# A graph network on one core: a relational layer's tail done in two parts, its fills moved, and a packing step moved behind the first layer

## The chip, the cores and the metric

The kernel runs on one core of a Trainium2 chip. The metric is the device time of one execution, in microseconds (us).

## What is computed

Four message-passing layers over 100,000 nodes of 32 features and 25,000 edges that come sorted by destination. Each layer normalizes, applies relu, aggregates over edges and adds to x:

```
h = relu(layernorm(x)); x = x + L0(h)   # norm * (segment_sum((norm*h)[src]) + norm*h)
h = relu(layernorm(x)); x = x + L1(h)   # four Chebyshev steps: feat += segment_sum(w * feat[dst])
h = relu(layernorm(x)); x = x + L2(h)   # relational attention, 86 edge types:
    msg = sum_b w_comp[etype, b] * (h[src] @ weight[b])
    a   = tanh(relu(sum((h[src]@A1 + b1) * (h[dst]@A2 + b2 + rel[etype])) / sqrt(32)))
    L2  = relu(segment_sum(a * msg, dst) + h[src of the node's last edge] @ self_loop)   # 0 without edges
h = relu(layernorm(x)); x = x + L3(h)   # ten steps: h = 0.9 * norm * segment_sum((norm*h)[src], dst) + 0.1 * h0
```

A node without edges gets only the parts of its own row, and in the last layer 0.1 * h0 goes into the output.

## The kernel before

**Columns.** The edges lie in 196 columns (`EC`) of 128 edges, one edge to a partition, so a table of all edges' rows is 128 x 6272 numbers (196 x 32). A segment sum is 32 running sums over the columns of a partition (`tensor_tensor_scan`, one for each feature) and one carry from partition to partition by TensorE.

**Rows in and out.** POOL fetches rows (`gather`, L1783) and writes rows (`scatter`, L1789) by indirect DMAs, one column of 128 rows each; an index beyond the bound drops its row. Nodes without edges ("dense" rows) pass through DVE and ScalarE in halves, and are written by plain DMAs of ScalarE's queue.

**The linked nodes.** After the segment sums, few rows matter to the later steps of layers 1 and 3: rows of nodes with edges whose source also has edges. Their lists are ranked, packed by matmuls against one-hot tiles (`spread`, L1118; `gathered_up`, L1148; `keyed`, L1028; `ranked`, L1049) and padded to 46, 12 and 4 columns. In the last layer the remaining steps work on one 128 x 128 matrix of links: a round of matmuls (L2271), two small DVE instructions, and again ("the rounds").

**Order of the work around the change.** Every engine runs its own program, in the written order, and waits on semaphores.

- DVE, layer 0: the lists of edges are made; the lists of nodes with several edges and of the edges that follow are packed (L1284 to L1295); then come dense halves, the norm of the sources (`source_norm`, L1349), `first_layer` (L1382) in three parts of the columns, and layer 1.
- Layer 2 is a loop of 49 turns of four columns (`l2_turns`, L1624). PE, ScalarE and DVE hand tiles to each other in it; DVE multiplies 128 x 512 products (L589) and reduces them over the 16 bases (L1602, `add_bases`), which raises the semaphore `l2_done` once a column. Behind the loop stands a tail over all 196 columns: the gate, the running sums (`segment_sums`, L982), the carry, relu and residual in pieces of 40 columns (`with_fed`, L633), then the copy of the rows into the table `own` (`OWNT`, L1646), which SP stores; zeros into `kept` (L1650, raises `l3_zero`); the layernorm; the table `first`, which SP also stores; and the rows `OUT` that are to be filled in.
- POOL during layer 2: 196 scatters of the source nodes' rows ("sends", L1901 to L1904), 12 of them free, the others one for each column done (`SENDS_AHEAD`). Behind the tail: 46 gathers from `own`, 46 from `first`, 38 fills, 12 + 12 gathers of the second list, 18 fills, 4 gathers of link rows; then the rounds with six fills in each of seven (`FILLS_TURN`, L1931); 4 scatters; 98 more fills; 46 + 12 last scatters. A "fill" (`fills`, L1912) writes a column of 0.1 * h0 plus residual for destination nodes that no later step touches; there are 196.

```
for k in range(L3_STEPS - 2):
    pool.wait_ge(s["link_turn_in"], k + 1)
    if k < L3_STEPS - 3:
        fills(early + FILLS_TURN * k, FILLS_TURN)
```

Of the kernel before, what the change touches and what calls it, by code (L numbers as in the profile page):

```python
# [8 lines left out]
D = 32  # L9
# [44 lines left out]
SENDS_AHEAD = 12  # L54
FILLS_LISTING, FILLS_PLACING, FILLS_TURN = 38, 18, 6
# [3 lines left out]
FEEDS = tuple((k, min(k + FEED, EC)) for k in range(0, EC, FEED))  # L59
UNROLL = 4  # L60
# [4 lines left out]
def build(nc, x, src, dst, etype, theta, w_basis, w_comp, w_self, a1t, a1b, a2t, a2b, rel, out):  # L65
# [33 lines left out]
    with ctx:  # L99
# [33 lines left out]
        def col(n):  # L133
            return c[n][:, 0:EC]
# [152 lines left out]
        v_at += W3 * ROWW  # L287
        V3, V3T = (rows(z_t[:, v_at + k * W3 * D:v_at + (k + 1) * W3 * D]) for k in range(2))
# [30 lines left out]
        def edge_layout(tile, at, nv, xw, wo):  # L319
# [92 lines left out]
            outd_scattered""".split()  # L412
# [31 lines left out]
        def _(sp):  # L444
# [116 lines left out]
            listed_tables("l3", OWNT, ((0, EC),))  # L561
# [22 lines left out]
        def _(dve):  # L584
# [697 lines left out]
            lead0, given0 = c["sq_out"][:, 100:100 + W0], c["sq_out"][:, 150:150 + W0]  # L1282
            link.many([ts(lead0, lead_p, -1.0, None, ALU.add), ts(given0, edge_p, -1.0, None, ALU.add)])
            spread(place0, receives, (ptr0, lead0, given0), W0, WM, MULTI)  # L1284
            ids = c["sq_out"][:, 0:3 * WM].rearrange("p (q v) -> p q v", v=3)
            gathered_up(ids, WM, 3, c["tmp"])
            many = slice(WS, W1)
            keyed(ids, WM, (pf0[:, many], owni[:, many], dst_slot[:, many]), contc[:, many], headc[:, many], wc[:], nohome[:, many])
            link(ts(valid1[:, many], ids[:, :, 1], 0.5, None, ALU.is_gt))

            place0 = ranked(follows, W0, WF)
            spread(place0, follows, (lead0, given0), W0, WF, FOLLOWING)
            ids = c["sq_out"][:, 0:2 * WF].rearrange("p (q v) -> p q v", v=2)
            gathered_up(ids, WF, 2, c["tmp"])
            pointers(ids, c["st2"][:, 0:2 * WF].rearrange("p (q v) -> p q v", v=2), ((0, leadF), (1, edgeF)))  # L1295
# [61 lines left out]
            dve.wait_ge(s["sums_scattered"], 16 * W0)  # L1357
            link(V.memset(kept[:, 0:kept_w], 0.0))
            V.memset(kept_keys, FAR).then_inc(s["l1_zero"], 1)
# [32 lines left out]
            for part in range(1, len(XS_PARTS)):  # L1392
                source_norm(part)
                first_layer(*XS_PARTS[part])
            dve.wait_ge(s["l1_own_ready"], len(XS_PARTS))
# [161 lines left out]
            link(V.tensor_copy(col("dst_out"), icols["outD"][:]))  # L1557

# [75 lines left out]
            ts(col("score"), col("score"), float(D) ** -0.5, 0.0, ALU.mult, ALU.max).then_inc(s["tail_ready"], 1)  # L1634
            dve.wait_ge(s["gate_made"], 1)
            link(tt(M, Z, bc(MEAN), ALU.mult))
            segment_sums(link, M, s["carry_in"], s["carry_out"], 1, None)
            V.memset(small[:, 2:3], 0.0).then_inc(s["tail_ready"], 1)

            def add_self(lo, hi, h):  # L1640
# [15 lines left out]
            link(tt(icols["outF"][:], col("dst_out"), col("tmp"), ALU.add))
            dve.wait_ge(s["outs_scattered"], 16 * EC)
            with_fed(lambda lo, hi, h: V.scalar_tensor_tensor(out=OUT[:, lo:hi, :], in0=h, scalar=ALPHA, in1=XD[:, lo:hi, :],
                                                              op0=ALU.mult, op1=ALU.add))
# [3 lines left out]
            dve.wait_ge(s["l3_first_ready"], 1)  # L1663
            dve.wait_ge(s["l3_first_stored"], 16)
            dve.wait_ge(s["l3_own_stored"], 16)
# [84 lines left out]
            with dve.Else():  # L1750
                ch = Chain(dve, s["dve"], before_end)
                dve.wait_ge(s["l3_listed_in"], 16 * w2)
                dve.wait_ge(s["l3_listed_stored"], 16)
                dve.wait_ge(s["l3_second_in"], 16 * w2)
                dve.wait_ge(s["l3_back_clear"], 16)
                layernorm_of(XD, F, Z, ch, roots("root_in", "root_out", root_count[0]))
# [20 lines left out]
        def _(pool):  # L1777
# [128 lines left out]
            pool.wait_ge(s["l3_own_stored"], 16)  # L1906
            gather(lambda k: OWN1[:, k, :], tables["l3", "own"], own3l, last[P * EC], s["l3_own_in"], W)
            pool.wait_ge(s["l3_first_stored"], 16)
# [6 lines left out]
            pool.wait_ge(s["d_rows_ready"], 1)  # L1915
            fills(0, FILLS_LISTING)
# [4 lines left out]
            early = FILLS_LISTING + FILLS_PLACING  # L1921
            fills(FILLS_LISTING, FILLS_PLACING)
            pool.wait_ge(s["fits_set"], 1)
            longest = pool.value_load(fits[0:1, 1:2], min_val=0, max_val=EC)
            with pool.If(longest <= XW):
                pool.wait_ge(s["l3_third_stored"], 16)
                gather(lambda q: GOT[:, q, :], links_dram, from3, last[P * w2], s["l3_third_in"], W3)
# [11 lines left out]
                pool.wait_ge(s["dfull_out"], 16 * EC)  # L1939
                pool.wait_ge(s["dc_out"], 16 * (W + w2))  # L1940
            with pool.Else():
# [7 lines left out]
                pool.wait_ge(s["dfull_out"], 16 * (FILLS_LISTING + FILLS_PLACING))  # L1949
# [6 lines left out]
        def _(act):  # L1956
# [21 lines left out]
            def feed(source):  # L1978

                act.wait_ge(s["normed"], norms[0])  # L1980
                for k, (lo, hi) in enumerate(FEEDS):
# [122 lines left out]
            l2_turns(0, EC // 4)  # L2104
            act.wait_ge(s["tail_ready"], 1)
            S.activation(MEAN, col("score"), ACT.Tanh).then_inc(s["gate_made"], 1)
            act.wait_ge(s["l2_cs"], EC)
            act.wait_ge(s["tail_ready"], 2)
            feed(XS)
            norm(XS, Z)  # L2110
            feed(Z)
# [191 lines left out]
```

## Time and profile before

| | |
|---|---|
| median of 3 runs | 2469.23 us (2468.75 to 2469.87) |
| profiled execution: its own time | 2470.35 us |
| its span in the profile | 2468.6 us |
| busy: DVE, POOL, ACT, PE, of the span | 1818.3 (74%), 1419.5 (58%), 388.7 (16%), 327.9 (13%) us |
| granted TensorE clock, mean over the span | 0.847 |

The span runs from the first to the last instruction that the profiler saw; the own time of that execution is 1.75 us longer. An engine's busy time says little by itself here: DVE and POOL are the bound in turn, each in stages of its own, so the profile has to be read by stage.

### The profile page before, as it was taken

The numbers are of one execution on the slowest core, as the hardware profiler recorded it, in microseconds if no ns is written. First come the engines' busy times: TensorE is split into PE (matmuls) and PEld (weight loads), VectorE is DVE, ScalarE is ACT, GpSimd is POOL, SyncE is SP. The second block draws the span as 40 slices with busy tenths as digits, with TensorE's granted clock in tenths as the row PEclk, the third lists the DMA queues.
The fourth block names the chain that finished last, engine by engine and source line by source line (L and its number), as shares of the span: only waits on it lengthen the run. The fifth ranks groups of instructions, "written<-read, shape, count | busy, mean of one in ns | idle before, by whom it ended". The sixth has DMA issues, their size and how long they took to land.

```text
span 2468.6 us, 12924 instructions
## 1 busy us (share of the span) xinstructions
PE 327.9 (13%) x2316; PEld 243.5 (10%) x2316; DVE 1818.3 (74%) x3200; ACT 388.7 (16%) x1275; POOL 1419.5 (58%) x1426
## 2 busy tenths in 40 slices
PE   0000000201100000010000001066764000034000
PEld 0000000101000000000000001044442000034000
DVE  8998989988699995971889989999999952321000
ACT  0000001010022121200112200177774210000000
POOL 6666776371776047306777720366662177777776
PEclk9999999999999999999999999976666555555555
DMA  1001003000221125100122220000000120100000
GB/s 21 17 9 29 12 16 119 6 12 2 96 66 32 51 67 178 42 34 10 63 71 62 84 77 0 3 8 8 8 8 4 59 69 10 35 12 11 8 8 8
DMA packets 57643, 88.37 MB, mean 36 GB/s; under 512 B 26387, under 2 KB 49864, under 8 KB 56184
## 3 DMA queue, kind: packets, MB, share of 16 engines
q0 software_dynamic: 44864, 19.00, 5.1%
q1 hardware_dynamic: 6872, 43.31, 4.5%
q10 hardware_dynamic: 5856, 25.60, 2.7%
q14 instruction: 46, 0.38, 0.1%
q8 instruction: 5, 0.08, 0.0%
HBM read 37.41 MB, written 54.76 MB: 37 GB/s over the span
## 4 chain that ended last, share of the span: by engine, by line
DVE 59%; POOL 15%; issue 12%; PE 6%; DMA 3%; ACT 2%; DVEq 0%; ACTq 0%; SPq 0%; POOLq 0%
POOL out L1789 9%; DVE mf L589 9%; POOL mf L1783 6%; DVE pay L589 4%; DVE psum L1321 4%; DVE pay L1307 4%; DVE psum L1306 3%; DVE outs L589 3%; DVE z L589 2%; PE psum L2271 2%; DVE z L1602 2%; DVE psum L618 2%; PE psum L2234 1%; DVE mf L1311 1%; DVE xs L1311 1%
## 5 line engine op out<-in xcount | busy, mean ns | idle before, releaser
L1789 POOL DMA_INDIRECT out<-outs,i_src x196 | 200.3, 1022 | 236.9 <-DVE outs L1578 109.2
L1783 POOL DMA_INDIRECT xd<-in_x,i_dst x196 | 205.2, 1047 | 109.7 <-DVE mf L589 55.5
L1783 POOL DMA_INDIRECT xs<-in_x,i_outS x196 | 195.9, 999 | 68.9 <-issue 56.4
L1789 POOL DMA_INDIRECT out<-outs,i_srcX x196 | 199.3, 1017 | 62.3 <-issue 57.6
L589 DVE TENSOR_TENSOR mf<-mf 128x128 f32<-128x128 f32 (+6 forms) x582 | 181.0, 348 | 10.5
L2005 ACT ACTIVATE pay<-pay 128x1248 f32<-128x1248 f32 (+1 forms) x63 | 75.6, 1199 | 647.4 <-DVE pay L1307 627.2
L589 DVE TENSOR_TENSOR pay<-psum,pay 128x512 f32<-128x512 f32 x196 | 130.4, 684 | 16.8 <-ACT pay L2095 14.7
L1602 DVE TENSOR_REDUCE z<-pay 128x512 f32 (+1 forms) x196 | 132.3, 675 | 0.0
L2234 PE MATMUL psum<-pay 128*128 128x512 f16 x196 | 102.7, 524 | 89.3 <-ACT pay L2080 55.6
L1783 POOL DMA_INDIRECT mf<-l_own_rows,lists x50 | 49.8, 996 | 111.9 <-DMA l_own_rows<-xs 97.0
L1783 POOL DMA_INDIRECT mf<-l_own_rows,ptr x46 | 45.9, 998 | 99.1 <-DMA l_own_rows<-pay 85.4
L1321 DVE SCALAR_TENSOR_TENSOR psum<-pay,psum 128x1248 f32<-128x1248 f32 (+1 forms) x63 | 88.7, 1407 | 2.2
L1789 POOL DMA_INDIRECT sums_by_edge<-mf,edge x46 | 45.3, 985 | 66.0 <-DVE mf L589 52.3
L1783 POOL DMA_INDIRECT mf<-l_second_rows,nsrc x26 | 26.0, 998 | 98.0 <-DMA l_second_rows<-mf 90.4
L2178 PE MATMUL psum<-lists,lower 128*128 128x32 f32 x4 | 1.3, 412 | 587.1 <-DVE lists L1189 587.1
L1306 DVE TENSOR_REDUCE psum<-outs 128x39 f32<-128x1248 f32 (+1 forms) x45 | 62.0, 1378 | 22.3 <-DMA outs<-in_x 21.8
L1783 POOL DMA_INDIRECT mf<-payload_by_dst,edge x46 | 45.8, 996 | 48.0 <-DVE mf L1225 34.3
L589 DVE TENSOR_TENSOR outs<-outs,psum 128x1248 f32<-128x1248 f32 (+2 forms) x55 | 68.5, 1258 | 1.6
L2224 PE MATMUL psum<-ident,pay 128*128 128x128 f16 x197 | 54.9, 279 | 92.0 <-ACT pay L2072 92.0
L1307 DVE SCALAR_TENSOR_TENSOR pay<-psum,outs 128x1248 f32<-128x1248 f32 (+1 forms) x45 | 62.1, 1381 | 1.6
L2148 PE MATMUL psum<-small,upper 128*128 128x1 f32 x18 | 5.3, 363 | 405.9 <-DVE small L1002 405.9
L2178 PEld LDWEIGHTS psum<-lists,lower 128*128 128x128 f32 x4 | 1.0, 312 | 587.4 <-DVE lists L1189 587.4
(521 smaller groups left out, 2726.2 us busy)
## 6 DMA issues: line engine op xcount, KB each, us to landing
outs<-in_x ACTq DMA_DIRECT2D x14, 624.0 KB, 5.4
out<-outs ACTq DMA_DIRECT2D x14, 624.0 KB, 3.0
l_first_rows<-mf SPq DMA_DIRECT2D x2, 3234.0 KB, 9.8
z<-in_x ACTq DMA_DIRECT2D x6, 624.0 KB, 6.0
out<-z ACTq DMA_DIRECT2D x6, 624.0 KB, 2.9
l_own_rows<-pay SPq DMA_DIRECT2D x1, 3430.0 KB, 9.5
payload_by_dst<-z SPq DMA_DIRECT2D x1, 3234.0 KB, 9.5
sums_by_edge<-z SPq DMA_DIRECT2D x1, 3234.0 KB, 17.3
```

The costliest lines, as they stand in the source:

```text
L589: return V.tensor_tensor(o, a, b, op)
L618: link(V.tensor_reduce(total, xin, AX.X, ALU.add))
L1306: chain(V.tensor_reduce(dense_m[b][0:pn, 0:cn], X3, AX.X, ALU.add))
L1307: V.scalar_tensor_tensor(out=rows(dxc[b][0:pn, 0:w]), in0=bc(dense_m[b][0:pn, 0:cn]), scalar=-1.0 / D, in1=X3, op0=ALU.mult, op1=ALU.add). ...
L1311: V.tensor_reduce(dst2[b][0:pn, 0:cn], rows(dsq[b][0:pn, 0:w]), AX.X, ALU.add).then_inc(s["dense_var"], 1)
L1321: chain(V.scalar_tensor_tensor(out=rows(h), in0=rows(dxc[b][0:pn, 0:w]), scalar=0.0, in1=bc(scale), op0=ALU.max, op1=ALU.mult))
L1602: V.tensor_reduce(Z[:, bass.ds(t, 1), :], prod[slot].rearrange("p (o b) -> p o b", b=NBAS).unsqueeze(1), AX.X, ALU.add).then_inc(s["l2_don ...
L1783: G.indirect_dma_start(out=dest(k), out_offset=None, in_=table, in_offset=bass.IndirectOffsetOnAxis(ap=idx[:, k:k + 1], axis=0), bounds_ch ...
L1789: G.indirect_dma_start(out=table, out_offset=bass.IndirectOffsetOnAxis(ap=idx[:, k:k + 1], axis=0), in_=source(k), in_offset=None, bounds_ ...
L2005: S.activation(dsq[b][0:pn, 0:w], dxc[b][0:pn, 0:w], ACT.Square).then_inc(s["dense_sq"], 1)
L2224: T.transpose(XXTp[b % 2], xxc[b], ident16[:])
L2234: T.matmul(PWm[b % 2], xxt[b], w_both, start=True, stop=True)
```

## The change

1. **Packing.** The packing of the two lists, and the zeros into layer 1's `kept`, move from ahead of the dense halves to behind the three `first_layer` parts. A copy of one small column (`place_m`) keeps what the packing reads.
2. **Two parts.** The loop of layer 2 is split after 24 turns (`CUT_TURN`), that is, after 96 columns (`CUT`). Between the two loops DVE does the tail for those 96 columns (slice `A`): the gate, running sums, relu and residual, the rows of `own` (in the tile `XSW`), the layernorm, the rows to be filled in (in `Z`) and the rows of `first`. Behind the second loop it does the other 100 columns (slice `B`), with column 95 (`HEADC`) again in the slice `BH`. The first segment of a partition, whose sum lacks the carry from the partition before, may end in the first part; its one row goes out by three extra scatters of one column each (into `own`, into `first`, and as a fill). Their indices, and those of the fills, are made by 19 short instructions ahead of layer 2.
3. **POOL's order.** Of the 196 sends 38 are free instead of 12, 40 are spread over DVE's work between the loops, and the others follow the columns done. Then 96 fills are issued, paced by the columns done, before the gathers from `own` start.
4. **No fills between the rounds.** `FILLS_TURN` is 0: of the 100 fills that are left, 38 and 18 stand where they stood, and 44 behind the rounds.

```diff
-SENDS_AHEAD = 12
-FILLS_LISTING, FILLS_PLACING, FILLS_TURN = 38, 18, 6
+SENDS_AHEAD = 38
+FILLS_LISTING, FILLS_PLACING, FILLS_TURN = 38, 18, 0
+CUT_TURN = 24
+CUT = 4 * CUT_TURN
+HEADC = CUT - 1
+SENDS_BETWEEN = 40
+OWN_BEFORE_HEAD = 36
...
-            spread(place0, receives, (ptr0, lead0, given0), W0, WM, MULTI)
...
-            pointers(ids, c["st2"][:, 0:2 * WF].rearrange("p (q v) -> p q v", v=2), ((0, leadF), (1, edgeF)))
+            place_m = end0
+            link(V.tensor_copy(place_m, place0))
...
                 source_norm(part)
                 first_layer(*XS_PARTS[part])
...
+            spread(place_m, receives, (ptr0, lead0, given0), W0, WM, MULTI)
...
+            V.memset(kept_keys, FAR).then_inc(s["l1_zero"], 1)
...
-            l2_turns(0, EC // 4)
+            l2_turns(0, CUT_TURN)
+            dve.wait_ge(s["l2_done"], CUT + 2)
...
+            gated(MA, A, 1)
+            running_sums(MA, A)
...
+            link(tt(Z[:, A, :], Z[:, A, :], CUR[:, A, :], ALU.add))
...
+            for given, out_row in ((Z, head_sum), (XD, head_own[:, 0:D])):
+                link(tt(MA, given[:, A, :], bc(ends), ALU.mult))
+                link(V.tensor_reduce(out_row, MA.rearrange("p c f -> p f c"), AX.X, ALU.add))
+            link(V.scalar_tensor_tensor(out=XD[:, A, :], in0=Z[:, A, :], scalar=0.0, in1=XD[:, A, :], op0=ALU.max, op1=ALU.add))
...
+            layernorm(XD[:, A, :], HA, MA, w=WA)
...
+            l2_turns(CUT_TURN, EC // 4)
...
+            gated(MB, B, 2)
...
+            running_sums(MB, B)
...
             for k in range(EC):
-                if k >= SENDS_AHEAD:
+                if k >= CUT + SENDS_AHEAD + SENDS_BETWEEN:
+                    pool.wait_ge(s["l2_done"], 3 + k - SENDS_AHEAD - SENDS_BETWEEN)
...
+            pool.wait_ge(s["d_rows_ready"], 1)
+            for k in range(CUT):
+                behind = EC - CUT - SENDS_AHEAD - SENDS_BETWEEN + k
+                pool.wait_ge(s["l2_done"], 2 + min(CUT + behind + 1, EC))
+                scatter(out, lambda q: Z[:, q, :], icols["outF"], last[N], s["dfull_out"], 1, k)
             pool.wait_ge(s["l3_zero"], 1)
```

POOL's program before, from the sends of layer 2 to the end (`out<-outs,i_src` are the sends, `i_srcX` the fills, `l_own_rows` and `l_first_rows` the tables, `z<-l_link_rows` the link rows of the rounds):

```order
L1789 DMA out<-outs,i_src 100000x32 x196
L1783 DMA mf<-l_own_rows,ptr 128x35 x46
L1783 DMA mf<-l_first_rows,ptr 128x33 x46
L1789 DMA out<-outs,i_srcX 100000x32 x38
...
L1789 DMA out<-outs,i_srcX 100000x32 x18
...
L1783 DMA z<-l_link_rows,linksi 128x33 x4
L1789 DMA out<-outs,i_srcX 100000x32 x42
L1789 DMA l_third_rows<-z,linksi 1536x32 x4
L1789 DMA out<-outs,i_srcX 100000x32 x98
```

The same stretch of POOL's program in the changed kernel:

```order
L1902 DMA out<-outs,i_src 100000x32 x196
L1902 DMA out<-z,i_srcX 100000x32 x96
L1902 DMA l_own_rows<-pay,edge 25088x35
L1896 DMA mf<-l_own_rows,ptr 128x35 x36
L1902 DMA l_first_rows<-mf,edge 25088x33
L1896 DMA mf<-l_own_rows,ptr 128x35 x10
...
L1902 DMA out<-outs,edge 100000x32
L1902 DMA out<-outs,i_srcX 100000x32 x38
...
L1896 DMA z<-l_link_rows,linksi 128x33 x4
L1902 DMA l_third_rows<-z,linksi 1536x32 x4
L1902 DMA out<-outs,i_srcX 100000x32 x44
```

96 fills moved ahead of the gathers from `own`, the 42 between the rounds are gone from there, and 44 instead of 98 stand behind; three scatters of one column are new.

DVE's program between the two loops of the changed kernel, where the kernel before has nothing (`score` and `psum` are the gate, `xd` the residual, `xs` the copy for `own`):

```order
L618 TENSOR_SCALAR score<-score 128x96
L615 TENSOR_TENSOR mf<-z,psum 128x3072
L1684 SCALAR_TENSOR_TENSOR z<-cont,mf 128x96 x32
...
L615 TENSOR_TENSOR mf<-z,tmp 128x3072
L1705 TENSOR_REDUCE chosen<-mf 128x32
...
L1706 SCALAR_TENSOR_TENSOR xd<-z,xd 128x3072
...
L1708 COPY xs<-xd 128x96x32
...
L656 SCALAR_TENSOR_TENSOR mf<-mf,psum 128x3072
L1712 SCALAR_TENSOR_TENSOR z<-mf,xd 128x3072
```

Instructions that ran over 196 columns behind the loop now run over 96 here, and over 100 or 101 behind the second loop.

## Rows read from the trace of the kernel before

**Rows 1.** Page part 4: shares of the chain that ended last, by engine.

```profile
DVE 59%; POOL 15%; issue 12%; PE 6%; DMA 3%; ACT 2%; DVEq 0%; ACTq 0%; SPq 0%; POOLq 0%
```

**Rows 2.** Windows: us; busy us (count) of PE, PEld, DVE, ACT, POOL; PEclk; DMA.

```profile
608.20:649.60 41.40, 6.98 (x98) 6.09 (x98) 32.21 (x67) 0.00 (x0) 31.32 (x32) 1.00 0.06 12
...
1596.70:1893.40 296.70, 202.46 (x1571) 133.52 (x1571) 279.78 (x543) 210.21 (x1084) 180.55 (x184) 0.70 0.04 7
1893.40:1951.10 57.70, 0.64 (x2) 0.50 (x2) 54.61 (x56) 6.32 (x6) 0.00 (x0) 0.50 0.00 0
...
2198.20:2253.10 54.90, 49.12 (x224) 48.17 (x224) 4.49 (x21) 0.00 (x0) 41.31 (x42) 0.50 0.04 8
2258.40:2385.20 126.80, 0.64 (x2) 0.50 (x2) 6.01 (x38) 0.00 (x0) 96.85 (x98) 0.50 0.05 9
```

**Rows 3.** Timeline, own rows to first gather: start, us, instruction, idle before.

```profile
1951.14 0.33 SPq L508 DMA_DIRECT2D l_own_rows<-pay  x1
1951.94 3.69 DVE L1650 MEMSET mf<- 128x4352 f32 x1 [0.82 <-issue]
...
1961.45 1.05 POOL L1783 DMA_INDIRECT mf<-l_own_rows,ptr  x1 [85.41 <-DMA l_own_rows<-pay]
```

**Rows 4.** Waits of POOL from 1961.4 on: total us, times, longest us.

```profile
POOL out L1789 <- issue: 75.2, 247, 0.3
```

**Rows 5.** Timeline of layer 1's start: the norm, POOL's gather, its first reader.

```profile
883.50 6.70 DVE L618 TENSOR_REDUCE psum<-xs 128x196 f32<-128x6272 f32 x1
887.60 0.99 POOL L1783 DMA_INDIRECT mf<-l_own_rows,lists  x1 [96.96 <-DMA l_own_rows<-xs]
...
1047.61 0.20 DVE L1422 COPY kc<-mf 128x50 f32<-128x50 f32 x1
```

**Rows 6.** Groups by form, DVE, 1893.2 to 1951.2: busy us, mean ns, idle.

```profile
L984 DVE TENSOR_TENSOR_SCAN z<-cont,mf 128x196 f32<-128x196 f32 x32 | 14.7, 542 | 0.0
L589 DVE TENSOR_TENSOR mf<-z,psum 128x6272 f32<-128x6272 f32 x1 | 6.7, 6689 | 0.4 <-ACT psum L2106 0.4
L1642 DVE SCALAR_TENSOR_TENSOR xd<-psum,xd 128x1280 f32<-128x1280 f32 x4 | 6.0, 1491 | 0.1
...
L589 DVE TENSOR_TENSOR z<-z,psum 128x2112 f32<-128x2112 f32 x2 | 4.7, 2353 | 0.1
L1646 DVE COPY pay<-xd 128x6272 f32<-128x6272 f32 x1 | 3.4, 3428 | 0.0
...
L592 DVE TENSOR_SCALAR score<-score 128x196 f32<-128x196 f32 x1 | 0.3, 262 | 0.1
```

**Rows 7.** Groups by form, DVE, 807 to 824: a layernorm over 104 columns.

```profile
L618 DVE TENSOR_REDUCE psum<-xs 128x104 f32<-128x3328 f32 x1 | 3.6, 3628 | 0.0
...
L628 DVE RECIPROCAL psum<-sq_out 128x104 f32<-128x104 f32 x1 | 0.8, 810 | 0.4 <-ACT sq_out L1975 0.4
```

**Rows 8.** Timeline: DVE's running sums over 46 columns, POOL's scatters beside them.

```profile
2083.37 4.60 DVE L1188 TENSOR_TENSOR_SCAN pay<-lists,mf 128x46 f32<-128x46 f32 x30
2084.47 4.34 POOL L1789 DMA_INDIRECT out<-outs,i_srcX  x1 [0.30 <-issue]
...
2089.12 0.98 POOL L1789 DMA_INDIRECT out<-outs,i_srcX  x1 [0.30 <-issue]
```

**Rows 9.** Timeline of DVE at the start of layer 2's loop.

```profile
1600.87 0.69 DVE L589 TENSOR_TENSOR pay<-psum,pay 128x512 f32<-128x512 f32 x1 [3.29 <-ACT pay L2095]
```

**Rows 10.** Windows of 10 us within layer 2's loop (columns as Rows 2).

```profile
1690.00:1700.00 10.00, 8.03 (x57) 5.31 (x55) 9.30 (x18) 6.66 (x38) 6.64 (x7) 0.51 0.04 8
1700.00:1710.00 10.00, 5.70 (x51) 3.76 (x50) 9.62 (x20) 7.37 (x38) 6.60 (x7) 0.83 0.04 8
```

**Rows 11.** Chain in order of time: start, us, the link rows' last transfer.

```profile
2195.28 2.35 DMA z<-l_link_rows,linksi
```

**Rows 12.** Timeline of one round of the links' matrix.

```profile
2198.06 7.04 PE L2271 MATMUL psum<-z,xs 128*128 128x32 f32 x32 [23.33 <-DVE small L1733]
...
2205.14 0.29 DVE L589 TENSOR_TENSOR z<-psum,z 128x128 f32<-128x128 f32 x1 [7.13 <-PE psum L2271]
```

More of the change, by code:

```diff
@@ L59, with feeds_of @@
 FEEDS = tuple((k, min(k + FEED, EC)) for k in range(0, EC, FEED))
+def feeds_of(first, last):
+    return tuple((k, min(k + FEED, last)) for k in range(first, last, FEED))
 UNROLL = 4
@@ L287, in build @@
         v_at += W3 * ROWW
+        head_own, head_sum = chosen[:, 0:OWNW], chosen[:, OWNW:OWNW + D]
+        cut_sum, cut_row = extra[:, 2 * W1:2 * W1 + D], extra[:, 2 * W1 + D:2 * W1 + 2 * D]
+        head_fill, head_row = edge0[:, 0:1], edge0[:, 1:2]
+        WA, WB = CUT, EC - HEADC
+        A, B, BH = slice(0, CUT), slice(CUT, EC), slice(HEADC, EC)
+        MA, HA = rows(mf[:, 0:WA * D]), rows(mf[:, WA * ROWW:WA * ROWW + WA * D])
+        HB = rows(z_t[:, CUT * D:CUT * D + WB * D])
+        assert WA * (ROWW + D) <= (CUT + 4) * 2 * D and CUT * D + WB * D <= EC * PAYLOAD
         V3, V3T = (rows(z_t[:, v_at + k * W3 * D:v_at + (k + 1) * W3 * D]) for k in range(2))
@@ L559, in _ @@
                 sp.dma_start(by_dst, xd_t[:]).then_inc(s["y_table"], 16)
-            listed_tables("l3", OWNT, ((0, EC),))
+            own_rows = tables["l3", "own"].rearrange("(p c) w -> p c w", p=P)
+            first_rows = tables["l3", "first"].rearrange("(p c) w -> p (c w)", p=P)
+            for k, (own, part) in enumerate(((XSW, A), (OWNT, B))):
+                sp.wait_ge(s["l3_own_ready"], k + 1)
+                sp.dma_start(own_rows[:, part, :], own[:, part, :]).then_inc(s["l3_own_stored"], 16)
+                sp.wait_ge(s["l3_first_ready"], k + 1)
+                span = slice(part.start * ROWW, part.stop * ROWW)
+                sp.dma_start(first_rows[:, span], first_f[:, span]).then_inc(s["l3_first_stored"], 16)
             sp.wait_ge(s["l3_cleared"], 1)
@@ L631, in layernorm, with with_fed @@
                 dve.wait_ge(s["normed"], norms[0])
-            def with_fed(step):
-                for k, (lo, hi) in enumerate(FEEDS):
+            def with_fed(step, parts=FEEDS):
+                for k, (lo, hi) in enumerate(parts):
                     dve.wait_ge(s["fed"], feeds[0] + 1)
@@ L1557, in _ @@
             link(V.tensor_copy(col("dst_out"), icols["outD"][:]))
+            ends, free = c["tmp"][:, A], c["tmp2"][:, 0:EC]
+            link(ts(free, col("kn"), FAR / 2, FAR, ALU.is_lt, ALU.mult))
+            link(tt(free, free, col("dst_out"), ALU.add))
+            link(V.tensor_copy(icols["outF"][:, B], free[:, B]))
+            link(V.scalar_tensor_tensor(out=icols["outF"][:, A], in0=c["head"][:, A], scalar=FAR, in1=free[:, A], op0=ALU.mult, op1=ALU.add))
+            link(tt(ends, c["head"][:, A], c["head"][:, 1:CUT + 1], ALU.subtract))
+            none, picked, found_at = c["st2"][:, 0:1], c["st1"][:, A], c["st2"][:, 1:2]
+            link(V.tensor_reduce(none, ends, AX.X, ALU.add))
+            link(ts(none, none, -FAR, FAR, ALU.mult, ALU.add))
+            for given, out_index in ((free[:, A], head_fill), (c["linear"][:, A], head_row)):
+                link(tt(picked, ends, given, ALU.mult))
+                link(V.tensor_reduce(found_at, picked, AX.X, ALU.add))
+                link(tt(out_index, found_at, none, ALU.add))
+            for k, name in enumerate(("dis", "kn", "dst_out")):
+                link(tt(picked, ends, c[name][:, A], ALU.mult))
+                link(V.tensor_reduce(head_own[:, D + k:D + k + 1], picked, AX.X, ALU.add))
             dve.wait_ge(s["dense_out"], 16 * (DCHUNKS + 1))
@@ L1629, in l2_turns, with gated, running_sums @@
                     l2_turn(last - 1, 0, False)
-            l2_turns(0, EC // 4)
+            def gated(out, part, number):
+                ts(c["score"][:, part], c["score"][:, part], float(D) ** -0.5, 0.0, ALU.mult, ALU.max).then_inc(s["tail_ready"], 1)
+                dve.wait_ge(s["gate_made"], number)
+                link(tt(out, Z[:, part, :], bc(MEAN[:, part]), ALU.mult))
+            def running_sums(m, part):
+                link.many([V.tensor_tensor_scan(Z[:, part, f], c["cont"][:, part], m[:, :, f], 0.0, ALU.mult, ALU.add) for f in range(D)])
@@ new lines, in own_rows @@
+            def own_rows(own, part):
+                link(V.tensor_copy(own[:, part, D], c["dis"][:, part]))
+                link(V.tensor_copy(own[:, part, D + 2], c["dst_out"][:, part]))
+                link(V.tensor_copy(own[:, part, D + 1], c["kn"][:, part]))
+            l2_turns(0, CUT_TURN)
+            dve.wait_ge(s["l2_scored"], CUT_TURN + 1)
+            dve.wait_ge(s["l2_done"], CUT + 2)
+            dve.wait_ge(s["l2_xy"], CUT_TURN + 1)
+            marks["cut"] = link.n
+            gated(MA, A, 1)
@@ new lines, in _ @@
+            link(V.scalar_tensor_tensor(out=XD[:, A, :], in0=Z[:, A, :], scalar=0.0, in1=XD[:, A, :], op0=ALU.max, op1=ALU.add))
+            link(V.tensor_copy(cut_row, XD[:, HEADC, :]))
+            link(V.tensor_copy(XSW[:, A, 0:D], XD[:, A, :]))
+            own_rows(XSW, A)
+            V.memset(small[:, 2:3], 0.0).then_inc(s["l3_own_ready"], 1)
+            layernorm(XD[:, A, :], HA, MA, w=WA)
+            V.scalar_tensor_tensor(out=Z[:, A, :], in0=HA, scalar=ALPHA, in1=XD[:, A, :],
+                                   op0=ALU.mult, op1=ALU.add).then_inc(s["d_rows_ready"], 1)
@@ L1638, in _ @@
+            dve.wait_ge(s["carry_out"], 1)
+            for lo, hi in SUM_CUT[1:]:
+                lo = max(lo, CUT)
+                added = rows(ADDED[:, 0:(hi - lo) * D])
+                link(tt(added, bf(CAR, hi - lo), bc(c["head"][:, lo:hi]), ALU.mult))
+                link(tt(Z[:, lo:hi, :], Z[:, lo:hi, :], added, ALU.add))
             V.memset(small[:, 2:3], 0.0).then_inc(s["tail_ready"], 1)
+            dve.wait_ge(s["l3_own_stored"], 16)
+            link(tt(head_sum, head_sum, CAR, ALU.add))
@@ L1640, in add_self @@
+            link(V.scalar_tensor_tensor(out=XD[:, HEADC, :], in0=head_sum, scalar=0.0, in1=head_own[:, 0:D], op0=ALU.max, op1=ALU.add))
             def add_self(lo, hi, h):
@@ L1913, in fills @@
                 scatter(out, lambda q: OUT[:, q, :], icols["outF"], last[N], s["dfull_out"], n, first)
-            pool.wait_ge(s["d_rows_ready"], 1)
-            fills(0, FILLS_LISTING)
+            pool.wait_ge(s["d_rows_ready"], 2)
+            scatter(out, lambda q: OUT[:, HEADC, :], head_fill, last[N], s["dfull_out"], 1)
+            fills(CUT, FILLS_LISTING)
             pool.wait_ge(s["l3_second_stored"], 16)
```

133 lines of the change are left out of this document (84 added, 49 removed).

## The prediction

> **What bounds the kernel now.** I read the chain that ended last first, then the windows by stage, then the groups and timelines of the stages that the change touches. The chain gives DVE 59% and POOL 15% [rows 1], and the windows show where one hands over to the other [rows 2]. Up to 1951.1 DVE sets the pace: it is busy 279.8 of 296.7 us in layer 2's loop and 54.6 of 57.7 in the tail. At 1951.1 the rows of `own` are complete and their store begins; 10.3 us later POOL's first gather starts [rows 3]. From there POOL works without a break to the end: before its scatters it only waits for issue, 0.3 us at the longest [rows 4], and the fills behind the rounds come at 126.8/98 = 1.294 us each [rows 2]. So two things count: when the first gather from `own` starts, and how many transfers POOL has to issue after it.
>
> All sums go against the profiled execution's own time, 2470.35 us (span 2468.6); the median of the runs is 2469.23, 1.12 lower, and I take that off at the end.
>
> **Packing moved: 0.2 us.** The stretch is 41.4 us with DVE busy 32.2; the rest is its waits for PE between its own steps [rows 2]. In the new place DVE does the same work with the same waits. Added is one small copy, 0.2. POOL's gather from layer 1's `own` starts 4.1 us behind the work that stands ahead of the norm, since it waits for a store [rows 5]; that store will now lie beside the packing. But the gather's first reader is DVE at 1047.6, without idle time [rows 5], so 160 us cover it; were that cover gone, its shift would count in full. The trace has no row for the swapped order, so I bound it by these 4.1 us to either side and take 0.
>
> **Indices ahead of layer 2: +5.0.** 19 short instructions at 0.262 [rows 6]; DVE is the pace there. Two of them leave a place beside POOL's gathers, where they cost nothing.
>
> **The work between the loops: +58.** Counted in DVE's program: 13 passes over 96 x 32 = 3072 numbers (gate; self row; two products and two reduces for the leading segment; relu with residual; four of the layernorm; fills; `first`). A pass costs 3.628/3328 x 3072 = 3.35 [rows 7], together 43.5. 32 running sums: 4.60/30 = 0.153 each over 46 columns [rows 8] and 14.7/32 = 0.459 over 196 [rows 6] give by a straight line 0.255 over 96, so 8.2. The copy for `own`: 3.43 x 96/196 = 1.7 [rows 6]. A reciprocal, 0.75 [rows 7], and nine small ones at 0.26: 3.1. ScalarE's tanh and root: 0.4 each [rows 6, 7]. Some 25 gaps of 0.035, as between DVE's instructions elsewhere: 0.9. Sum 58.2. Bounds: the two reduces walk with a stride that no row shows; between the 3.35 of a contiguous one and its double I take the former, +6.7 at most and nothing below. The second loop may begin with the 3.29 that DVE waited at the first start [rows 9]; here PE and ScalarE have 58 us to fill their tiles ahead, so I take 0, +3.3 at most.
>
> **The loop itself: 0.** PE now rests for 58 us in its middle. The granted clock swings within the loop anyway, 0.51 in one window of 10 us and 0.83 in the next (the levels are 1.2 and 2.4 GHz), while DVE is busy 9.30 and 9.62 [rows 10]. So a window at the slow level costs 0.32 in 10 us at most. For the 100 columns behind the cut, half of 296.7 = 151 us, that bounds the price at 0.032 x 151 = 4.8 if the clock stays low throughout. At the loop's mix it is 0, which I take, for the clock rises in this loop without help.
>
> **The tail behind the loop: 57.7 to 33.0, so -24.7.** Over 100 of 196 columns the gate takes 3.4 instead of 6.7, the running sums 8.4 instead of 14.7; relu and residual, two passes at 1491/1280 ns a number, 7.5 instead of 14.6; the carry, two passes at 2353/2112, 7.1 instead of 14.0; the copy 1.8 instead of 3.4 [rows 6]. Waits, 57.7 - 54.6 = 3.1 [rows 2], stay, and so do small ones, with the leading segment's 1.7.
>
> Together the rows of `own` are ready 0.2 + 5.0 + 58.2 - 24.7 = 38.7 later, near 1990.
>
> **From there to the first gather: 10.3 to 7.4, so -2.9.** Before, the store set it, 10.3 us, beside 4.5 us up to the end of the zeros into `kept` [rows 3]. Now the last store is half as long, some 5 by proportion; the zeros (4.6), then the leading segments' scatter until it has landed (2.35 for a column's transfer [rows 11]) and an issue gap set it. First gather: +35.8, near 1997.
>
> **POOL afterwards: -67.3.** Two more scatters of leading segments: 2 x 1.294 = +2.6. The gathers and the 38 + 18 fills stay. **In the rounds,** a round is 7.04 us of PE, seven times, and DVE waits for PE's last matmul each time, not for POOL [rows 12]; so the 42 fills that leave them save nothing there, and POOL will stand idle for most of 55 us. Behind the rounds 44 fills stand where 98 stood: 54 x 1.294 = -69.9. Put otherwise: of the 96 fills that leave POOL's last stretch, 42 had been free.
>
> Row against rule: PE is busy 49.1 of these 54.9 us at a granted 0.50 throughout, the level of 1.2 GHz, while it was granted 1.00 from 608 to 650, where it worked 7 of 41 us [rows 2]. So I leave the rounds at 7.04. The Trainium skill ("TensorE: Matmul & The Clock Gate", Part 1: The HAM clock gate) has it that the slow level is the default and sustained activity lifts it; by that the rounds would run at the fast level, which rival 1 works out. This trace does not agree.
>
> **Does the backlog fit?** The 96 fills are free only if POOL is through with them when the zeros are ready, near 1994.6. Some of DVE's passes hold POOL's transfers up: a scatter that takes 0.98 took 4.34 beside the running sums and ended with the last of them [rows 8]. Between the loops I put such passes at half of the 58 us, so 28 of the 40 sends get done there. 12 + 22 sends and 96 fills are left for the second loop and the tail, 1805 to 1994.6. In the loop a transfer is not held up: 180.55/184 = 0.98 [rows 2]. A column takes 1.51, so POOL catches the 12 up at 0.2 a column, in some 75 columns, and ends the loop, at 1956, with the 19 fills that wait for its end: 19 x 1.29 = 24.5, and 10 of holding up by the tail's sums, 1990.5. It fits by 4 us. That is the weakest step.
>
> **Sum:** +35.8 + 2.6 - 69.9 = -31.5: own time 2438.9, against the median 2437.7. **I predict 2438.** With the bounds above (-4.1 to +4.1, +6.7, +3.3, +4.8, not all at once) this case alone reaches from 2432 to 2450.
>
> **Rivals.**
>
> 1. *Rounds at the fast level.* PE's rest in mid-loop shifts the sequence of levels; at 2.4 GHz each round would lose up to 7.04/2, seven of them 24.6: 2413. For it: the clock moves both ways in the loop [rows 10]. Against: 0.50 through all rounds [rows 2]. Chance 0.05.
> 2. *A mild backlog.* If a transfer takes p in the second loop and tail, 130 of them and the 10 of holding up have 189.6 us; they fit up to p = 1.38. At p of 1.45 to 1.50 the first gather moves by 9 to 15: 2447 to 2453. For it: passes that hold POOL up [rows 8]. Against: 0.98 in the loop, 1.29 from start to start behind the rounds [rows 2]. Chance 0.11.
> 3. *The other side: a backlog that eats the gain.* The first gather stands behind all 96 fills in POOL's program, so each that is late counts in full. From p = 1.62 (130 x 1.62 + 10 is 31 over) the kernel is slower than before; at 1.75 the first gather is 48 late: 2486. It needs DVE's 128 x 512 products to hold POOL up once it is driven closer, which the loop before doesn't show. Chance 0.04.
> 4. *The fills between the rounds weren't free,* if they slowed PE or DVE there. DVE's wait of 7.13 is PE's own 7.04 and 0.09 [rows 12], and the sum of the rounds, 54.9, is 5.8 over PE's 49.1 [rows 2]: at most that is won, 2432. Chance 0.05.
> 5. *The dense work gains or loses by its earlier start,* beside other transfers of POOL than before, 4 to 10: most likely a gain, 2428 to 2434. Chance 0.05.
>
> **How the numbers follow.** My case has 0.70. The low end of the range takes in rivals 4 and 5 and leaves rival 1 out, 2425; the high end takes the bounds and rival 2, 2455. A measurement of this kernel tells 0.2% (5 us) from no change, so same is 2464 to 2474. All cases but rival 3 are faster; a little of its chance and of rival 2's may fall within 0.2%: faster 0.94, same 0.02, slower 0.04.
>
> **What would show it.** Right: DVE's work between the loops 56 to 62 us; a tail of 33; the first gather from `own` at 1994 to 2002, released by the landing of the leading segments' scatter; the rounds still 7.9 each with POOL idle; 44 fills behind them at 1.29. Wrong: fills still running when the zeros are ready (rivals 2, 3); a granted clock over 0.50 in the rounds (rival 1); more than 70 us between the loops.

## The result, and the profile after

The changed kernel takes 2456.31 us (median of 4 runs, 2454.13 to 2456.60) against 2469.55 (4 runs, 2468.75 to 2471.24) for the kernel before on the same chip: ratio 0.9942, 95% interval 0.993 to 0.9955. It is faster by 13 us (0.6%), where 31.5 were forecast, and 1.3 us above the upper end of the range. The profiled execution took 2456.60, its span is 2454.8.

The windows of the changed kernel, in order: the first loop, DVE's work between the loops, the second loop, the tail, from the own rows to the first gather, the fills behind the rounds, and last the rounds themselves (columns as in [rows 2]):

```profile
1607.70:1755.75 148.05, 104.95 (x782) 68.89 (x782) 137.95 (x271) 104.83 (x534) 107.52 (x109) 0.67 0.05 9
1755.75:1817.50 61.75, 1.30 (x8) 0.76 (x8) 60.26 (x61) 7.92 (x20) 44.95 (x34) 0.52 0.10 34
1817.50:1967.10 149.60, 103.31 (x781) 67.96 (x781) 141.84 (x276) 104.36 (x536) 104.91 (x107) 0.66 0.07 19
1967.10:2002.30 35.20, 0.64 (x2) 0.50 (x2) 32.44 (x55) 3.35 (x4) 19.04 (x20) 0.50 0.03 6
2002.30:2010.30 8.00, 0.00 (x0) 0.00 (x0) 7.09 (x4) 0.00 (x0) 1.03 (x2) 0.50 0.54 226
2310.30:2367.40 57.10, 0.63 (x2) 0.50 (x2) 6.05 (x38) 0.00 (x0) 43.69 (x45) 0.50 0.05 11
2249.50:2304.90 55.40, 48.86 (x224) 47.92 (x223) 4.51 (x21) 0.00 (x0) 0.00 (x0) 0.50 0.00 0
```

The last row is the rounds: 55.4 us with POOL at 0 transfers, against 54.9 with 42 [rows 2], at the same granted 0.50. The two loops together take 297.65 against 296.7, so the cut neither disturbs nor helps them. The loop starts at 1607.7; before, the stretch of the loop began at 1596.7: 11 us are lost before layer 2, where 5.2 were forecast.

Around the own rows, the timeline of the changed kernel answers to [rows 3]:

```profile
2002.36 0.32 SPq L584 DMA_DIRECT2D l_own_rows<-pay  x1
2003.19 3.69 DVE L1750 MEMSET mf<- 128x4352 f32 x1 [0.86 <-issue]
2007.30 0.98 POOL L1902 DMA_INDIRECT l_own_rows<-pay,edge  x1 [15.36 <-DVE mf L1751]
2010.25 1.05 POOL L1896 DMA_INDIRECT mf<-l_own_rows,ptr  x1 [1.97 <-DMA l_own_rows<-pay,edge]
```

POOL was through with the fills and stood idle for 15.4 us before the zeros released it: there is no backlog. But the own rows are there at 2002.3, not near 1990, and the first gather comes 48.8 later than before, not 35.8.

By stage, both profiled executions compared (span 2468.6 and 2454.8; what lies ahead of layer 2 is read from how much later DVE starts the same instruction):

| step of the forecast | forecast, us | measured, us |
|---|---|---|
| packing moved | +0.2 | +5.8 |
| indices ahead of layer 2 | +5.0 | +5.3 |
| loops | 0 | +0.9 |
| between the loops | +58.2 | +61.75 |
| tail | -24.7 | -22.5 |
| own rows to first gather | -2.9 | -2.3 |
| first gather to POOL's last transfer | -67.3 | -66.6 |
| from there to the end | 0 | +4.0 |
| sum | -31.5 | -13.65 (spans: -13.8) |

### The profile page after: what moved, and what is told of

It is laid out like the page before. It is cut to its first block and busy times, and to the rows that moved or that the text cites. A ratio compares the mean times of both kernels' runs of the same rounds, so it can differ in the third digit from the quotient of the medians.

```text
span 2454.8 us, 13021 instructions
## 1 busy us (share of the span) xinstructions
PE 334.9 (14%) x2316; PEld 247.7 (10%) x2316; DVE 1839.1 (75%) x3276; ACT 387.0 (16%) x1277; POOL 1445.5 (59%) x1429
## 5 line engine op out<-in xcount | busy, mean ns | idle before, releaser
L1902 POOL DMA_INDIRECT out<-outs,i_src x196 | 222.9, 1137 | 186.8 <-DVE outs L1623 113.0
L1902 POOL DMA_INDIRECT out<-outs,i_srcX x100 | 104.4, 1044 | 30.5 <-issue 30.5
L1902 POOL DMA_INDIRECT out<-z,i_srcX x96 | 94.4, 984 | 41.6 <-DVE z L1647 24.8
L2102 ACT ACTIVATE outs<-pay 128x3136 f32<-128x3136 f32 x6 | 16.9, 2817 | 274.6 <-DVE pay L646 274.6
L1902 POOL DMA_INDIRECT x_rows<-mf,lists x50 | 50.7, 1014 | 15.2 <-issue 15.2
```

The lines of the kernel that those rows point to most:

```text
L1902: G.indirect_dma_start(out=table, out_offset=bass.IndirectOffsetOnAxis(ap=idx[:, k:k + 1], axis=0), in_=source(k), in_offset=None, bounds_ ...
L2102: S.activation(hout[:, side, :], tmp[:, side, :], ACT.Square).then_inc(s["norm_squared"], 1)
```

## The experiments

Each experiment is compared with runs of the kernel before on its own chip, whose medians lie between 2469.5 and 2471.3; so a difference between the times of two experiments carries up to 2 us of that, and the ratios do not.

**What made the moved packing dear.** Ahead of layer 1 the timeline of the changed kernel shows one idle time that the kernel before does not have, in the dense halves that now start 42 us earlier:

```profile
667.86 3.65 ACTq L2166 DMA_DIRECT2D out<-outs  x2
668.27 0.32 SPq L543 DMA_DIRECT2D z<-sums_by_edge  x1
...
683.76 2.38 ACT L2135 ACTIVATE pay<-pay 128x1248 f32<-128x1248 f32 x2 [18.87 <-DMA out<-outs]
685.04 2.81 DVE L1325 TENSOR_REDUCE mf<-pay 128x39 f32<-128x1248 f32 x2 [8.18 <-ACT pay L2135]
```

ScalarE writes out the first dense half and waits until that has landed before it loads the third; SP starts to reload the table of sums 0.4 us after this store. ScalarE's squares come late, and DVE waits 8.18 us for them. The DMA issues of the changed kernel from 660 to 690 (KB each, us to landing) give the two transfers:

```profile
z<-sums_by_edge SPq DMA_DIRECT2D x1, 3234.0 KB, 14.2
out<-outs ACTq DMA_DIRECT2D x2, 624.0 KB, 7.8
```

The 7.8 is the median of the two transfers that store a half. One by one (issues from 667 to 669, then from 669 to 672), the second, which ScalarE has to wait for, took 11.7:

```profile
out<-outs ACTq DMA_DIRECT2D x1, 624.0 KB, 3.8
...
out<-outs ACTq DMA_DIRECT2D x1, 624.0 KB, 11.7
```

In the kernel before, the reload ran from 671, behind the first dense loads, and the first store came at 711; its two transfers took 2.9 and 3.0:

```profile
671.36 0.32 SPq L524 DMA_DIRECT2D z<-sums_by_edge  x1
...
711.14 3.66 ACTq L2036 DMA_DIRECT2D out<-outs  x2
```

Theory A: the loss is this meeting. The packing by itself, on the kernel before:

```diff
-            spread(place0, receives, (ptr0, lead0, given0), W0, WM, MULTI)
...
                 first_layer(*XS_PARTS[part])
+            spread(place_m, receives, (ptr0, lead0, given0), W0, WM, MULTI)
```

> The kernel before with the packing and the zeros of layer 1 moved behind the first layer, and nothing else. Theory A (the loss comes from the moved packing: the reload of the table of sums, 3.2 MB, now meets the second store of the dense halves, and ScalarE, which waits for that store, holds DVE up by 8 us): slower than before by 4 to 6 us, about 2474.5, with one idle time of DVE of some 8 us behind the second dense half. Rival (as the prediction had it, the move costs 0.2 and the loss seen before layer 2 comes from the other parts): 2469 to 2470.

Measured: 2476.99 against 2471.28, ratio 1.0023 (1.0013 to 1.0033), and DVE waits 7.4 us in one piece for ScalarE behind the second dense half. The move by itself is a loss; the rival that priced it at 0.2 falls. The reverse, the changed kernel with the packing in its old place:

> The changed kernel with the packing and the zeros of layer 1 in their old place. Theory A: 5 to 6 us less than the changed kernel, 2450 to 2451, own rows of the last layer ready 5 us earlier. Rival (the move is worth nothing): 2456. A third view (the move is worth something of its own that another loss hides): more than 2457.

Measured: 2449.18 (2448.77 to 2452.97), ratio to the kernel before 0.991 (0.9897 to 0.9924). By the timelines DVE reaches layer 1's norm 4.6 us earlier; the medians say 7. The profiled execution was the slowest of the five, 2452.97, only 3.6 under that of the changed kernel, so the spread of these runs covers the difference. Whether it is the meeting or the packing's new place, one line tells:

```diff
             sp.wait_ge(s["sums_scattered"], 16 * W0)
+            sp.wait_ge(s["dense_out"], 16 * 3)
             sp.dma_start(z_t[:], by_edge).then_inc(s["sums_in"], 16)
```

> The changed kernel in which SP starts the reload of the table of sums only when the second dense store is out. Theory A (collision): DVE's 8.2 us of idle time behind the second dense half falls to under 1 and the time to 2448 to 2450. Rival B (the moved packing itself is dearer in its new place, or the dense halves are late for another reason): 2456, with the idle time still there. If the reload then holds up its reader, DVE idles ahead of the first layer instead.

Measured: 2448.70 (2447.19 to 2450.81), ratio 0.9907 (0.9892 to 0.9922). The timeline of this kernel at the same place:

```profile
674.76 0.85 ACTq L2156 DMA_DIRECT2D outs<-in_x  x2
674.82 0.32 SPq L544 DMA_DIRECT2D z<-sums_by_edge  x1
675.66 1.24 ACT L2136 ACTIVATE pay<-pay 128x1248 f32<-128x1248 f32 x1 [10.37 <-DMA out<-outs]
675.80 1.46 DVE L1322 SCALAR_TENSOR_TENSOR pay<-psum,outs 128x1248 f32<-128x1248 f32 x1
677.18 2.84 DVE L1326 TENSOR_REDUCE mf<-pay 128x39 f32<-128x1248 f32 x2
```

ScalarE now waits 10.4 us for its store instead of 18.9 (the two transfers land in 2.9 and 3.2), DVE not at all; DVE is 7.9 us earlier from there on, and the first gather from `own` 7.3. The reload itself now meets the load of the third half, which takes 13.4 us instead of 4.6, and nobody waits for that one. Theory A holds. With the collision gone, the runs do not tell the packing's new place from its old one: 2448.7 against 2449.2. The timeline gives the new place a little: DVE starts layer 1's norm at 881.1, 2.4 us ahead of the kernel before, and 8.2 less 2.4 is the 5.8 of the table.

**The fills in the rounds.**

```diff
-FILLS_LISTING, FILLS_PLACING, FILLS_TURN = 38, 18, 0
+FILLS_LISTING, FILLS_PLACING, FILLS_TURN = 38, 18, 6
```

> The changed kernel with FILLS_TURN 6 again: 42 of the 44 fills go back between the rounds. If the fills there are covered by PE's 7.04 us and lost that cover by the change: 42 x 1.294 = 54 us less than the changed kernel, about 2402, with the rounds still 7.9 us each. Rival (the fills slow the rounds, so that taking them out gave something back): the rounds grow by up to 6 us together and the time is 2403 to 2408.

Measured: 2403.32 (2402.04 to 2403.69), ratio 0.9722 (0.9707 to 0.9737): 53 us less than the changed kernel from one number. The time lies between the two cases (2402, and 2403 to 2408), so the rounds have to decide. Timeline of a round of this kernel, and of the changed kernel without fills:

```profile
2250.73 7.04 PE L2405 MATMUL psum<-z,xs 128*128 128x32 f32 x32 [22.93 <-DVE small L1838]
2250.95 1.03 POOL L1902 DMA_INDIRECT out<-outs,i_srcX  x1 [2.02 <-DVE small L1838]
...
2257.80 0.29 DVE L615 TENSOR_TENSOR z<-psum,z 128x128 f32<-128x128 f32 x1 [7.13 <-PE psum L2405]
```

```profile
2249.10 7.04 PE L2405 MATMUL psum<-z,xs 128*128 128x32 f32 x32 [22.85 <-DVE small L1838]
2256.17 0.29 DVE L615 TENSOR_TENSOR z<-psum,z 128x128 f32<-128x128 f32 x1 [7.13 <-PE psum L2405]
```

PE takes 7.04 and DVE waits 7.13 with six fills beside a round as without: the rounds did not grow. The fills were free there, and the change gave 53 of the 121 us away that its 96 early fills are worth behind the rounds (96 x 1.29 less the 2.6 of two more scatters).

**Four mendings together, and what the room holds.** The groups of the changed kernel (DVE from 1755.7 to 1817.5, then from 1967 to 2002.4) show the two places at which DVE's work was dearer than forecast:

```profile
L1705 DVE TENSOR_REDUCE chosen<-mf 128x32 f32<-128x3072 f32 x2 | 10.6, 5275 | 0.1
L1684 DVE TENSOR_TENSOR_SCAN z<-cont,mf 128x96 f32<-128x96 f32 x32 | 8.1, 329 | 0.0
...
L644 DVE TENSOR_REDUCE psum<-xd 128x96 f32<-128x3072 f32 x1 | 3.4, 3355 | 0.0
...
L1746 DVE COPY pay<-xd 128x3232 f32<-128x3232 f32 x1 | 3.5, 3522 | 0.0
```

The strided reduce takes 5.28 where the contiguous one over as many numbers takes 3.36, and the copy of 101 columns takes longer than that of 196 before [rows 6]. The Trainium skill ("VectorE: DVE Perf Modes", What auto-detection actually checks) lets a copy within SBUF run at double speed only where the outermost dimensions of source and destination, those of one element left out, are both even or equal. Here the source is one run of 3232 numbers, the destination 101 pieces of 32; by that rule 101 pieces go at single speed, and the row agrees with 1.09 ns a number, against 0.55 before. The rule goes by the number of pieces; the copy also starts at column 95 here and at column 0 before, and no run changes the one without the other.

```diff
-            link(V.tensor_copy(OWNT[:, BH, 0:D], XD[:, BH, :]))
+            link(V.tensor_copy(OWNT[:, B, 0:D], XD[:, B, :]))
+            link(V.tensor_copy(OWNT[:, HEADC, 0:D], XD[:, HEADC, :]))
...
-            pool.wait_ge(s["l3_zero"], 1)
             pool.wait_ge(s["l3_own_ready"], 2)
             scatter(tables["l3", "own"], lambda q: OWNT[:, HEADC, :], head_row, last[P * EC], s["heads_out"], 1)
+            pool.wait_ge(s["l3_zero"], 1)
```

> The changed kernel with four things mended at once: six fills in each round again, the reload behind the second dense store, the leading segments' scatter into own ahead of the wait for the zeros, and the copy of the rows into own from column 96 on (column 95 by itself). If the four losses are separate, they add up: 2403.3 (fills back in the rounds) - 7.6 (reload later, as measured) - 1.2 to -2.9 (the gather starts when the store of own rows has landed instead of 8.0 us behind them) - 1.7 (the copy of 101 columns took 3.5 us, that of 196 before 3.4: a copy that starts on an even column should take half): 2391 to 2393. Rival (the losses cover each other, since POOL's fills of the first part then end too late for an earlier gather): 2396 or more, with fills still running when the own rows are ready.

Measured: 2392.16 (2390.79 to 2392.31), ratio 0.9679 (0.9663 to 0.9695). The four add up. From this kernel's DVE groups, the copies:

```profile
L1747 DVE COPY pay<-xd 128x3200 f32<-128x3200 f32 x1 | 1.8, 1828 | 0.0
...
L1748 DVE COPY pay<-xd 128x32 f32<-128x32 f32 x1 | 0.2, 182 | 0.0
```

2.0 for both in place of 3.5. Then eight more columns ahead of the cut:

```diff
-CUT_TURN = 24
+CUT_TURN = 26
-FILLS_LISTING, FILLS_PLACING, FILLS_TURN = 38, 18, 6
+FILLS_LISTING, FILLS_PLACING, FILLS_TURN = 34, 14, 6
```

> As the kernel with four things mended, but the cut after 26 turns, 104 columns, so that eight more fills run beside layer 2, and 34 and 14 fills before the rounds. POOL stood idle for 15 us ahead of the own rows in the changed kernel, which is room for 11 fills. If that room holds: 8 x 1.29 = 10 us less, 2381 to 2383. Rival (the backlog binds): the paced fills end behind the own rows and the first gather waits for them; 2384 to 2392, with POOL busy without a gap up to that gather.

Measured: 2386.57 (2385.43 to 2389.11), ratio 0.9661 (0.9645 to 0.9677): the rival's case. In the timeline of this kernel POOL is still at its fills when the own rows are stored, at 1995.3:

```profile
1995.32 0.32 SPq L585 DMA_DIRECT2D l_own_rows<-pay  x1
1995.39 0.99 POOL L1904 DMA_INDIRECT out<-z,i_srcX  x1 [0.30 <-issue]
...
2000.55 0.98 POOL L1904 DMA_INDIRECT l_own_rows<-pay,edge  x1 [0.30 <-issue]
2003.52 1.05 POOL L1898 DMA_INDIRECT mf<-l_own_rows,ptr  x1 [1.99 <-DMA l_own_rows<-pay,edge]
```

So the room is there, but the pace by columns done leaves 27 transfers for the time behind the loop. Own rows are 1.7 us later than in the kernel with four mended, and from there to the first gather it takes 8.2 us instead of 6.5. Without that pace:

```diff
-                pool.wait_ge(s["l2_done"], 2 + min(CUT + behind + 1, EC))
```

> The same with 104 columns, and the fills of the first part not paced by the columns done. If the pace only delays them, they end earlier, POOL idles ahead of the own rows, and the time is that of the paced one or less, 2379 to 2383. Rival (transfers at POOL's own pace disturb DVE's loop): the loop grows from 1.51 us a column and the time is above the paced one's.

Measured: 2385.27 (2383.82 to 2386.37), ratio 0.9654 (0.9637 to 0.967). POOL ends its fills nearly 6 us before the own rows, and the first gather comes at 2001.86 instead of 2003.52. The difference in time, 1.3 us, is less than the runs can tell; the loop was not disturbed.

**The strided reduce.** On that kernel, three additions of halves and a reduce over 13 columns in place of each:

```diff
-                link(V.tensor_reduce(out_row, MA.rearrange("p c f -> p f c"), AX.X, ALU.add))
+                half = CUT // 2
+                while half >= 13:
+                    link(tt(MA[:, 0:half, :], MA[:, 0:half, :], MA[:, half:2 * half, :], ALU.add))
+                    half //= 2
+                link(V.tensor_reduce(out_row, MA[:, 0:13, :].rearrange("p c f -> p f c"), AX.X, ALU.add))
```

> The kernel with 104 columns and free fills, in which the two strided reduces over 104 columns (5.70 us each) are done as three additions of halves, quarters and eighths and a reduce over 13 columns. If the stride is what makes the reduce dear (1.7 ns a number against 1.09 of a contiguous one): 1664 + 832 + 416 numbers at 1.09 and 416 at 1.7 are 3.9 in place of 5.70, so 3.5 us less in all, about 2382. Rival (the reduce is dear for its 32 results, not for its stride, or own rows no longer set the pace): 2384 to 2386.

Measured: 2381.61 (2380.09 to 2382.46), ratio 0.9641 (0.9625 to 0.9657). From this kernel's timeline of DVE:

```profile
1782.15 3.58 DVE L616 TENSOR_TENSOR mf<-mf 128x1664 f32<-128x1664 f32 x3
1785.77 0.85 DVE L1710 TENSOR_REDUCE chosen<-mf 128x32 f32<-128x416 f32 x1
```

4.46 in place of 5.70, a gain of 1.2 for each and not the 1.8 expected, and the first gather comes 1.7 us earlier. What makes the reduce dear can be read from its two sizes (the first line is of the kernel with 104 columns and unpaced fills, the others of this one):

```profile
L1706 DVE TENSOR_REDUCE chosen<-mf 128x32 f32<-128x3328 f32 x2 | 11.4, 5702 | 0.1
```

```profile
L645 DVE TENSOR_REDUCE psum<-xd 128x104 f32<-128x3328 f32 x1 | 3.6, 3623 | 0.0
...
L653 DVE TENSOR_REDUCE sq_in<-mf 128x52 f32<-128x1664 f32 x1 | 1.9, 1886 | 0.0
...
L1710 DVE TENSOR_REDUCE chosen<-mf 128x32 f32<-128x416 f32 x2 | 1.7, 848 | 0.1
```

Both strided reduces have 32 results; 2912 numbers more cost 4.85 us, 1.67 ns a number, and leave only 0.15 us as a fixed part. For the contiguous ones 1664 numbers more cost 1.74 us, 1.04 ns a number. So the price goes by the numbers read with the stride and not by the 32 results. The additions took 3.58 and not the 3.2 expected, since each of the three has a fixed part too (the one over 416 numbers took 0.59).

This is the fastest version that was run, 3.6% below the kernel before; its interval overlaps with that of the one before it.

**The longer end.** The source view of POOL's last line gives the closing drain, for the kernel before and the one after:

```profile
L99 POOLq DRAIN  x1: 4807/4807/4807, 2463.5 to 2463.5; - x1
```

```profile
L110 POOLq DRAIN  x1: 8727/8727/8727, 2445.9 to 2445.9; - x1
```

3.9 us of the missing gain lie behind all work. It was 8.73 in every kernel with the two parts and 4.81 in every other. Four tries at its cause:

```diff
+                pool.wait_ge(s["dfull_out"], 16 * early)
+                fills(0, 3)
                 fills(early, EC - early)
```

> The kernel before with three fills issued twice, all else as it was: 199 fills. It tells what the longer end is: POOL's closing drain took 4.81 us in the kernel before and in the one with the packing moved, 8.73 in the changed kernel and in all that have its two parts and its three extra scatters. If the drain goes by the number of transfers: 8.73 here, and the time 3 x 1.29 + 3.9 = 7.8 over the kernel before. If it goes by something else in the two-part program: 4.81 and 3.9 over.

Measured: drain 4.81, 2474.66 against 2470.88 (ratio 1.0016, 1.0007 to 1.0026): not the number of transfers.

```diff
-            scatter(tables["l3", "own"], lambda q: OWNT[:, HEADC, :], head_row, last[P * EC], s["heads_out"], 1)
...
-            scatter(tables["l3", "first"], lambda q: FIRST[:, HEADC, :], head_row, last[P * EC], s["heads_out"], 1)
...
-            scatter(out, lambda q: OUT[:, HEADC, :], head_fill, last[N], s["dfull_out"], 1)
```

> The changed kernel without its three scatters of leading segments; those rows are left out of the output, and out of the tables. It tells what lengthened the closing drain. If the drain goes by these scatters (each a transfer of a single column with its own indices): 4.81 and a time of 2456 - 3.9 (two of the scatters, the wait for the landing 2.0 before the gather, less what the own rows' store then sets) - 3.9 = about 2446 to 2449. If it goes by something else in the two-part program: 8.73 again, and about 2450 to 2453.

Measured: drain 8.73, one run of 2450.38: not these scatters.

```diff
+            for k in range(100):
+                pool.wait_ge(s["outs_ready"], 1)
             pool.wait_ge(s["l3_zero"], 1)
```

> The changed kernel with 100 waits added to POOL's program, all for a semaphore that is long set, where POOL stands idle for 15 us ahead of the own rows. The work is the same, only the program is longer. If the closing drain (8.73 us in every kernel with the two parts so far) goes by where in the program POOL stands at its end, it changes here; if it goes by the work, it stays at 8.73. The time otherwise that of the changed kernel.

> The kernel before with the same 100 waits at the same place, where POOL stood idle for 85 us. If the drain goes by the program's length or place, 4.81 changes here, most likely towards 8.73; if by the work of the two parts, it stays at 4.81.

Measured: 8.73 (one run, 2456.69) and 4.81 (2473.23): not the length of the program. What sets the drain stays open; the second loop with its waits and the added semaphore, which only the kernels with two parts have, were not taken out by themselves.

## Why the prediction was wrong

The direction, the mechanism and most terms came out; the size did not. 17.9 us of the forecast gain are missing, 15.3 of them in four steps.

- **"Packing moved: 0.2 us."** Failed: +5.8, outside the bounds of 4.1 to either side. The moved work itself was no dearer in the new place, as argued: without the collision the move is worth -2.4. But with it the dense halves moved by 42 us, and SP's reload, which waits for POOL, by only 3 (from 671.4 to 668.3), so that the two met and DVE lost 8.2. I weighed the moved step and POOL's gather, and not the transfers of the steps that stay and now start earlier. ScalarE's stores and SP's reload had no row in the working. Rival 5 named the start of the dense work, but beside POOL's transfers and with a gain as the likely sign. The experiments show the cause: the packing alone costs it, and one wait on SP gives it back.
- **"From there to the end."** I had no term; the closing drain took 3.9 more. Cause open.
- **"The work between the loops: +58."** Mis-sized: 61.75. The two strided reduces took 5.28 each and not 3.35; 3.9 of the 6.7 that the bound allowed. The other passes came within 0.15 us of their rows, the running sums at 8.1 against 8.2 from the straight line.
- **"The tail behind the loop: -24.7."** Mis-sized by 2.2, of which 1.7 are the copy, which I took in proportion to its columns; 101 columns took 1.09 ns a number, 196 had taken 0.55.

What held:

- *POOL afterwards:* -66.6 against -67.3. That the 42 fills of the rounds had been free is shown by the run with six a round again: 53 us, against 54 worked out, with PE's 7.04 the same.
- *The loop* kept its pace across the cut. Rival 1 did not happen: the granted clock in the rounds stayed at 0.50.
- *Backlog.* Fills ended at 1991.9 against 1990.5 worked out, and that agreement is luck: the loop ended 11 us later than assumed (1967.1 against 1956), and the 10 us for which the tail's sums were to hold POOL up did not come. The backlog was to fit by 4 us and fitted by 15, since the own rows were late. Rivals 2 and 3 did not happen; with 104 columns and the pace the backlog did bind, by 1.7 us.
- *Own rows to the first gather:* released by the landing of the leading segments' scatter, as said, 8.0 against 7.4.

The backlog's term of 10 us rested on one transfer that took 4.34 beside running sums [rows 8]; it ended 0.8 us behind them, not with them. In the tail of the changed kernel every transfer beside 8.4 us of running sums took 0.98:

```profile
1971.64 8.38 DVE L1684 TENSOR_TENSOR_SCAN z<-cont,mf 128x100 f32<-128x100 f32 x32
...
1971.64 0.98 POOL L1902 DMA_INDIRECT out<-z,i_srcX  x1 [0.30 <-issue]
1972.92 0.98 POOL L1902 DMA_INDIRECT out<-z,i_srcX  x1 [0.30 <-issue]
```

## What to carry to other kernels

When a step is moved, list the transfers of everything that thereby starts earlier, on every queue, and look what they meet; an engine that waits for its own store to land passes the delay on. Before work is taken out of a gap, see what covered it: 42 transfers beside a waiting PE were free, and behind it cost 53 us. A pass is not priced by its number of elements alone: take a row of the same stride and, for copies, one with a number of columns that is even or odd as well.

## What the runs showed of the hardware

- The mean granted clock of a whole execution says nothing of its time here: the four runs of the changed kernel had 0.848, 0.693, 0.696 and 0.694 at 2456.60, 2456.07, 2456.55 and 2454.13 us.
- A reduce over a stride of 32 numbers took 1.72 ns a number against 1.09 for a contiguous one over as many; by the two sizes of each, 1.67 against 1.04 without the fixed part. The Trainium skill ("SBUF — State Buffer", Door 1: The DMA port swizzle) has it that accesses which leave a 16-byte line each time pay a penalty, without a figure for DVE; the rows agree.
- A store of 624 KB that took 3.0 us to land in the kernel before took 11.7 beside a reload of 3.2 MB, and the engine that waited for it passed 8.2 us on.
- Running sums over 100 columns did not hold up POOL's transfers (0.98 us each, as without), where one beside those over 46 columns took 4.34 [rows 8]; between the loops five of POOL's transfers took 3.0 to 4.5. Why they differ is open.
- POOL's closing drain is 4.81 or 8.73 us, the same to 0.01 in all profiled executions of a kind, and none of four changes moved it.
